# Cross-attention in a fused perceiver kernel: the row of maxima and the second half of the scores moved behind the third key chunk, next to the weighing

## The reference, cut to what matters

```python
q = split_heads(layernorm(x) @ Wq)            # 16 batches x 16 heads x 64 x 32
k = split_heads(ctx @ Wk)                     # 16 x 16 x 1601 x 32
v = split_heads(ctx @ Wv)
attn = softmax(einsum('bhid,bhjd->bhij', q, k) * SCALE, axis=-1)
out = einsum('bhij,bhjd->bhid', attn, v)
x = x + merge_heads(out) @ Wp + bp
...
```

## Time and profile before

| | |
|---|---|
| Median of three runs | 1918.98 us (1917.98 to 1925.94) |
| The profiled execution | 1919.2 us |
| Its span in the profile | 1917.4 us |
| TensorE busy | 1849.8 us, 96% |
| VectorE busy | 1116.4 us, 58% |
| ScalarE busy | 834.6 us, 44% |
| GpSimd busy | 873.9 us, 46% |

### The profile page before, as it was taken

The page is one execution under the profiler, slowest core; times in us unless marked ns, Lnnn a source line. Parts: engine busy times, 40 slices in busy tenths (PEclk is TensorE's granted clock), DMA queues, the critical chain, the costliest instruction groups (busy, mean ns, idle before and its releaser), DMA issues. The chain is left out here.

```text
span 1917.4 us, 65530 instructions
## 1 busy us (share of the span) xinstructions
PE 1849.8 (96%) x28992; PEld 1595.3 (83%) x28992; DVE 1116.4 (58%) x1354; ACT 834.6 (44%) x1032; POOL 873.9 (46%) x830
## 2 busy tenths in 40 slices
PE   6999999999999999999999999999999989789998
PEld 3979898989888888888888989898989768667887
DVE  4475665657474848384848474747475561763265
ACT  4444444545453535353535353545444413334322
POOL 0293636454554546372728282828272620544211
PEclk9999999999999999999999999999999989789999
DMA  5200202011010202020202020202020140222110
GB/s 211 85 4 3 76 3 76 16 64 45 34 68 12 77 2 77 3 77 3 76 3 76 3 76 3 76 3 76 3 75 3 67 133 23 46 72 91 52 56 23
DMA packets 38829, 94.54 MB, mean 49 GB/s; under 512 B 18593, under 2 KB 18593, under 8 KB 38305
## 3 DMA queue, kind: packets, MB, share of 16 engines
q1 hardware_dynamic: 38560, 90.26, 13.3%
HBM read 81.99 MB, written 6.16 MB: 46 GB/s over the span
## 5 line engine op out<-in xcount | busy, mean ns | idle before, releaser
L379 POOL TENSOR_TENSOR fold<-fold,prob 128x256 f32<-128x256 f32 (+1 forms) x704 | 700.3, 995 | 55.2
L98 PE MATMUL ring<-y_parts,wk_s 128*128 128x402 f32 (+1 forms) x3072 | 607.4, 351 | 1.4 <-PEq L152 1.4
L98 PE MATMUL ring<-wv_s,y_parts 128*128 128x512 f32 (+1 forms) x2496 | 596.2, 396 | 0.0
L98 PEld LDWEIGHTS ring<-y_parts,wk_s 128*128 128x128 f32 x3072 | 551.1, 188 | 17.4 <-issue 4.1
L98 PEld LDWEIGHTS ring<-wv_s,y_parts 128*128 128x128 f32 (+1 forms) x2496 | 453.8, 184 | 112.6
L373 POOL TENSOR_TENSOR fold<-prob 128x256 f32<-128x256 f32 x64 | 68.2, 1066 | 698.0 <-ACT prob L416 698.0
L393 ACT ACTIVATE k_sb<-ring 128x402 f32<-128x402 f32 (+1 forms) x256 | 129.4, 505 | 372.5 <-PE ring L98 372.5
L525 DVE TENSOR_TENSOR prob<-prob,peak_rows 128x1024 f32<-128x1024 f32 (+1 forms) x192 | 277.9, 1499 | 12.2 <-ACT peak_rows L412 12.2
L406 ACT ACTIVATE prob<-s_ps 128x1536 f32<-128x1536 f32 (+1 forms) x128 | 199.9, 1561 | 128.0 <-PE s_ps L642 128.0
L416 ACT ACTIVATE prob<-prob 128x1024 f32<-128x1024 f32 (+1 forms) x192 | 207.5, 1123 | 3.2 <-DVE prob L525 1.3
L502 DVE TENSOR_TENSOR fold<-prob 128x512 f32<-128x512 f32 x64 | 51.8, 809 | 228.2 <-ACT prob L406 228.2
(11 more groups left out here) (142 smaller groups left out, 1474.7 us busy)
## 6 DMA issues: line engine op xcount, KB each, us to landing
y_raw<-yT SPq DMA_DIRECT2D x48, 804.0 KB, 5.8
y_raw<-yT SPq DMA_DIRECT2D x16, 792.0 KB, 9.9
f_raw<-w_ffn SPq DMA_DIRECT2D x22, 512.0 KB, 3.2
p_x<-x SPq DMA_DIRECT2D x2, 1024.0 KB, 7.2
q_scratch<-p_x SPq DMA_DIRECT2D x4, 512.0 KB, 2.7
q_sb<-q_scratch SPq DMA_DIRECT2D x16, 128.0 KB, 8.5
x_sb<-x SPq DMA_DIRECT2D x4, 512.0 KB, 6.1
v_sw<-y_raw SPq DMA_DIRECT2D x4, 512.0 KB, 8.5
```

The lines of the kernel that those rows point to most:

```text
L98: mm = pe.matmul(out, left(a, c), right(b, c), start=(c == 0 and n == 0), stop=(c == DC - 1 and n == 2))
L379: pool.tensor_tensor(acc[0:m], acc[0:m], prob[0:m, i, t, :], ALU.add).then_inc(sum_step, 1)
```

## The change

In TensorE's order, for blocks 2 and 3, chunk 2 is moved ahead of the spreading and the second half of the scores. ScalarE's order is changed to match: the copy of chunk 2 comes ahead of the row of maxima and of the second score copy. VectorE's, GpSimd's and the DMA orders are the same as before, and no instruction is added or removed.

```diff
@@ ScalarE, keys_phase, blocks 1 to 3
                     score(b, i - 1, 0)
                     key(b, i, 1)
                     if i >= 2:
+                        key(b, i, 2)
                         peak_row(b, i - 2)
                     score(b, i - 1, 1)
-                    key(b, i, 2)
+                    if i < 2:
+                        key(b, i, 2)
                     if i >= 2:
                         exponential(b, i - 2, 0)
                         exponential(b, i - 2, 1)
@@ TensorE, batch, blocks 2 and 3
                     turn(b, i - 2)
                     scores(b, i - 1, 0)
                     keys(b, i, 1)
+                    keys(b, i, 2)
                     spread_peaks(b, i - 2)
                     scores(b, i - 1, 1)
-                    keys(b, i, 2)
                     if past:
                         small_rows(b, i - 2)
                         weigh(b - 1, i)
```

## The result

The changed kernel takes 1998.74 us (median of four runs, 1994.33 to 2000.3) where the kernel before took 1919.99 beside it: 1.040 times as long, 95% interval 1.0382 to 1.0418. The forecast was 1979, with a range of 1955 to 2010. The direction held, and so did the length of VectorE's chain behind the waits. But half of the foreseen waits did not appear: stops of TensorE inside the weighing, which the forecast had priced at nothing, took their place, and they account for about 15 us of what the forecast was short.

What follows compares the result with a forecast made beforehand. TensorE, 96% busy, was taken as the bound. Waits of 2.96 and 1.11 us, less 0.15 saved per block, gave 3.77 us a batch; sixteen batches add 60.3 to 1919.2: 1979 us, range 1955 to 2010.

Steps and rivals of the forecast that it cites:

- foreseen waits: TensorE at the turn, waiting for VectorE's output: 2.96 us in block 2 and 1.11 in block 3 of each batch.
- What bounds the kernel, and that nothing is given back: TensorE, busy 96% of the span: idle time inserted in steady batches is paid in full and never given back.
- The chain from the spreading: VectorE's subtraction, maxima and output, blocks 2 and 3: ends +10.70 us after the spreading's start, turn at +10.85.
- The first batch: No weighing or output there: each wait grows by 0.9 us, but 1.82 was already paid, so again about 3.8.
- "I take 0" for the move from the scores straight into the weighing: TensorE, blocks 2 and 3: this new change-over costs between -0.27 and +0.27 us per block, taken as 0.
- a small gain: TensorE, blocks 2 and 3: chunk 2 directly behind chunk 1 takes 2.25 us instead of 2.40, saving 0.15 per block.
- the chain's times: Spreading to turn near 10.85 us in both blocks, first GpSimd addition about 4.6 behind the spreading, three subtractions 3.7.
- the thirty waits in two sizes: TensorE's list of waits should show some 30 for VectorE's output, near 3.0 and 1.1 us.
- The clock: Rival, chance 0.10: TensorE's clock falls to half behind block 2's 2.96 us wait, 61 us in all, 2040 us.
- the faster one: Rival, chance 0.04: only the joining counts, in blocks 2 and 3, saving 5 to 13 us, 1906 to 1914.
- GpSimd came at +4.50, not late: Rival, chance 0.06: GpSimd's sum starts behind the maxima, block 2 waits 0.82 us, block 3 none; 8 us, 1927.
- VectorE and GpSimd taking strict turns: Rival, chance 0.04: each of five maximum steps waits for a whole 0.85 us GpSimd addition; 62 us more, 2041.

Runs made afterwards that it cites:

- e1: The changed kernel with the weighing moved behind chunk 3 in blocks 2 and 3, away from the second scores: 2014.28 us, ratio 1.0492.
- e4: The changed kernel with only the weighing's first 32 matmuls directly behind the scores, the rest behind chunk 3: 2001.03 us, ratio 1.044.
- e5: The changed kernel with padding matmuls at the head of each batch, 80 matmuls and 160 instructions by the trace: 2077.8 us in one run.
- e2: The kernel before with the weighing directly behind the second scores and chunk 2 behind it, the spreading left in place: 1968.54 us, ratio 1.0261.
- e7: The kernel of e1 with GpSimd's sum cut to its first addition in every block: 1938.73 us in one run.
- e10: The kernel of e1 with VectorE's second maxima and output ahead of the subtraction, ScalarE's exponentials behind its copy of chunk 3: 1977.76 us, ratio 1.03.
- e6: The kernel of e2 with redundant waits ahead of key chunks, 80 added instructions a batch by the page: 2019.69 us, ratio 1.0523.

## Why the prediction was right, and where it was not

*What bounds the kernel, and that nothing is given back:* right. From one pass of TensorE's loop to the next it is 97.33 us on average, where it was 92.54: a batch is 4.8 us longer (3.8 in the forecast), some 77 us for sixteen of the 80.2, and no later stage made it up.

*The chain from the spreading:* right to a few hundredths. Subtraction at +1.01, maxima at +4.69, end at +10.70, turn at +10.83 against +10.85. That VectorE's output ended only 0.55 and 0.21 us ahead of the turn before, and that the distance shrank by a whole chunk, was enough to know it. e1 and e4, which have no such stops, and e5, which has one, show the two waits at 2.43 to 2.75 and 0.67 to 1.02 us of idle.

*The first batch:* its two waits are 2.78 and 1.99 us, where the forecast had 0.9 more than in a later batch, 3.9 and 2.0. In block 2 the first exponential comes at +4.80 (83.77 - 78.97), behind a table load of 1.28 us on ScalarE, so GpSimd comes at +5.94 and the maxima have less of its company.

*"I take 0" for the move from the scores straight into the weighing:* this is the step that failed. It was bounded by 0.27 us on either side from the idle time ahead of a weight load, and it cost 1.23 and 2.08 us. The bound came from the change of weights and left out that instructions themselves have to arrive. The error in the sum is smaller than that, because a stop delays TensorE within the distance in which it would have waited anyhow. In block 2 the stop and the wait together cost 1.23 + 1.71 = 2.94, and the forecast had 2.96 for the wait alone. In block 3 the stop's 2.08 took the place of 1.11. So 0.97 us a batch were missing, 15 us.

*What was luck:* the total came within 20 us because two costs overlapped that the forecast did not weigh against each other. The joining alone costs 48 us (e2), where the forecast had a small gain. The waits for VectorE without the stops, with the clock that falls behind them, cost 94 us (e1), where it had 60. Of the signs that the forecast named, the chain's times came, while the thirty waits in two sizes did not.

*The clock:* named as a rival at 0.10, with the remark that it would fall at some of the waits. It fell six times inside the cross-attention, twice in the first batch and in four later ones. In one batch the stretch from the resumed weighing to the first value tile takes 783.67 - 778.96 = 4.71 us at partly half clock and 881.97 - 878.78 = 3.19 in another at full clock: 1.5 us, or 9 for six, an estimate from one of them. 60 + 15 + 9 makes 84 us against the measured 80.2, and the two-chunk runs take up to 3 off, being 0.2 us shorter than two single chunks and not 0.15; a stop's idle time alone varies between 0.83 and 1.79 us from batch to batch.

```profile
778.96 1.23 PE L677 MATMUL small_ps<-prob,v_sb 128*32 128x64 f32 x42 [1.75 <-issue]
...
783.67 2.94 PE L98 MATMUL ring<-wv_s,y_parts 128*128 128x512 f32 x12
```

The forecast saw the clock stay up around a wait of 1.82 us and asked about one of 2.96. The changed kernel shows the low clock behind a wait of 1.39 us too, at 1548.91, with a stop of 1.00 us earlier in the batch.

*The rivals:* the faster one is out, its saving being real but 0.15 to 0.2 us per block; GpSimd came at +4.50, not late, and e7, where it hardly runs, still waits 0.92 us a batch; VectorE and GpSimd taking strict turns did not appear, maxima and output taking 6.01 us.

What stays open is which idle pattern lets the clock fall. It fell after every 2.6 us wait in e1, in 9 of 15 later batches of e4, in most of e5 and e10, in 4 of the changed kernel, and not after the single 0.9 us waits of e7. How TensorE chooses the moment of a fetch was not studied either; in the loop of e5 many fetches come in pairs, 30 to 120 instructions apart, with up to 480 to the next pair.

## What to carry to other kernels

Where the bounding engine shows no wait, read how far behind it the others are at each hand-off: a chain that ends 0.5 us early turns a move of 2.4 us into a wait of about 2 us in every iteration. Count from the event that starts the chain, not from the end of the list. On TensorE, where this was measured, do not put two long runs of very short instructions next to each other: the saved change-over is tenths of a microsecond, and an instruction fetch that falls into the run can stop it for one to two; with a long matmul group between them the fetch is hidden.

## What was not expected of the hardware

- TensorE stops for its own instructions. It goes on 1.22 to 1.58 us behind the end of a 16 KB fetch that takes 0.88 to 1.45 us, and the profile calls the time "issue". 160 instructions added 35 us earlier removed 29 of 30 stops (e5).
- Removing those stops made the kernel slower: e1 takes 2014 us and the changed kernel 1999. Each of its uninterrupted waits of 2.6 us is followed by a clock of 0.50, which a stop and a shorter wait are in only 4 of 15 later batches.
- A redundant wait on TensorE is not free: 80 wait instructions a batch show as some 55 us of "issue" in 68 places ahead of the key chunks (e6).
